# A depthwise 5x5 convolution as 24 tiles of 126 pixels, turned around the middle pixel, instead of 25 squares of 11x11

## What is computed

```python
k = jnp.transpose(kernel, (1, 2, 0))[:, :, None, :]
y = lax.conv_general_dilated(x, k, window_strides=(1, 1), padding='SAME',
                             dimension_numbers=('NHWC', 'HWIO', 'NHWC'), feature_group_count=ch)
return x + y
```

## Time and profile before

| | us |
|---|---|
| median of 3 runs | 827.06 |
| lowest, highest | 826.73, 827.2 |
| the profiled execution | 826.83 |
| its span | 825.0 |
| TensorE busy | 814.7 |
| VectorE busy | 670.8 |
| ScalarE busy | 619.6 |
| GpSimd busy | 591.9 |

### The profile page before, as it was taken

One profiled execution on the slowest core, in us unless ns is written; L12 is line 12 of the kernel. 1 busy time (PEld: TensorE's weight loads), 2 busy tenths in 40 slices (PEclk: granted clock), 3 DMA queues, 4 the chain that ended last, 5 costly groups with the idle time before them and its releaser, 6 DMA issues.

```text
span 825.0 us, 20812 instructions
## 1 busy us (share of the span) xinstructions
PE 814.7 (99%) x7200; PEld 814.5 (99%) x7200; DVE 670.8 (81%) x2118; ACT 619.6 (75%) x1538; POOL 591.9 (72%) x389
## 2 busy tenths in 40 slices
PE   6999999999999999999999999999999999999998
PEld 6999999999999999999999999999999999999998
DVE  6888888878788887878888888878888887888886
ACT  5777777777777777777777777777777777777775
POOL 6768577696775867858668677685775867758662
PEclk9999999999999999999999999999999999999999
DMA  9999999999999999999999999999999999999975
GB/s 364 414 388 402 354 395 375 376 381 367 402 371 376 384 371 395 376 368 400 355 382 398 368 400 363 373 397 356 401 372 378 353 404 384 377 365 405 363 317 227
DMA packets 28759, 309.29 MB, mean 375 GB/s; under 512 B 3184, under 2 KB 3312, under 8 KB 4208
## 3 DMA queue, kind: packets, MB, share of 16 engines
q1 hardware_dynamic: 28656, 307.98, 97.1%
HBM read 158.55 MB, written 149.42 MB: 373 GB/s over the span
## 4 chain that ended last, share of the span: by engine, by line
PE 99%; POOL 0%; DMA 0%; issue 0%; ACT 0%; DVE 0%; DVEq 0%
PE sums L419 66%; PE sums L415 33%; POOL matrix L237 0%; DMA first<-consts 0%; POOL expanded L228 0%; POOL taps L219 0%; POOL spare L216 0%; POOL taps L214 0%; ACT y_out L307 0%; DVE y_out L357 0%; DVEq L95 0%
## 5 line engine op out<-in xcount | busy, mean ns | idle before, releaser
L419 PE MATMUL sums<-matrix,x_high 121*128 121x240 f32 (+3 forms) x4800 | 814.2, 278 | 0.0
L419 PEld LDWEIGHTS sums<-matrix,x_high 121*128 121x128 f32 x4800 | 730.7, 192 | 0.0
L415 PE MATMUL sums<-matrix,x_low 121*128 121x240 f32 (+3 forms) x2400 | 665.8, 277 | 6.8 <-POOL matrix L237 6.8
L307 ACT ACTIVATE y_out<-sums 128x220 f32<-128x220 f32 (+6 forms) x1248 | 420.5, 376 | 194.3 <-PE sums L419 175.8
L357 DVE TENSOR_TENSOR y_out<-sums,y_out 128x60 f32<-128x60 f32 (+5 forms) x1824 | 358.8, 227 | 144.6 <-ACT y_out L307 62.6
L415 PEld LDWEIGHTS sums<-matrix,x_low 121*128 121x128 f32 x2400 | 460.4, 192 | 6.9 <-POOL matrix L237 6.8
L265 POOL TENSOR_TENSOR x_low<-x_in,x_high 121x640 fp32r<-121x640 f32 x190 | 320.7, 1710 | 119.0 <-DVE x_high L331 119.0
L340 DVE TENSOR_TENSOR x_low<-x_in,x_high 121x1280 fp32r<-121x1280 f32 (+1 forms) x194 | 290.2, 1497 | 2.2 <-ACT x_high L297 2.1
L297 ACT ACTIVATE x_high<-x_in 121x640 fp32r<-121x640 f32 (+1 forms) x288 | 263.6, 916 | 7.3 <-DMA x_in<-x 7.3
L253 POOL TENSOR_TENSOR matrix<-expanded,mask 121x600 fp32r<-121x600 f32 x95 | 157.9, 1662 | 92.4 <-PE sums L419 90.5
L331 DVE CAST x_high<-x_in 121x640 fp32r<-121x640 f32 x96 | 68.1, 710 | 3.8 <-DMA x_in<-x 3.3
(11 more groups left out here) (5 smaller groups left out, 0.6 us busy)
## 6 DMA issues: line engine op xcount, KB each, us to landing
x_in<-x SPq DMA_DIRECT2D x95, 1600.0 KB, 10.2
y<-y_out SPq DMA_DIRECT2D x95, 1520.0 KB, 13.2
rest<-later SPq DMA_DIRECT2D x1, 1150.0 KB, 12.1
x_in<-x SPq DMA_DIRECT2D x3, 320.0 KB, 3.6
y<-y_out SPq DMA_DIRECT2D x1, 852.5 KB, 3.6
x_in<-x SPq DMA_DIRECT2D x1, 640.0 KB, 6.1
y<-y_out SPq DMA_DIRECT2D x1, 365.0 KB, 2.3
y<-y_out SPq DMA_DIRECT2D x1, 302.5 KB, 2.7
```

The costliest lines, as they stand in the source:

```text
L307: act.activation(outputs(c, rows, cols), sums(c, t, rows, cols), ACT.Copy).then_inc(copied, 1)
L415: pe.matmul(target, x_low[c % SLOTS][0:PIXELS, at:at + IMAGES], window(c, strip, k, slice(HIGH, HIGH + 1)).squeeze(1), start=k == tile["sq ...
L419: product = pe.matmul(target, x_high[c % SLOTS][0:PIXELS, at:at + IMAGES], window(c, strip, k, slice(part, part + 1)).squeeze(1), start=Fa ...
```

## The change

The plane is cut into 24 tiles of 14x9 = 126 pixels instead of 25 squares of 121. Four quarters, each 28 x 27, turn around the middle pixel like the blades of a wheel; two hold lying tiles (FLAT, 9 rows by 14 columns), two standing ones (TALL, 14 by 9). The middle pixel itself, which no quarter covers, is a 127th pixel of one tile. So there are 72 matmuls a channel, 6912 in all, and two matrices a channel, one for each kind of tile. The columns of the moving operands sum up to 5270 a channel per matmul of the three, against 5396 before.

- Two tiles share a bank: 12 banks a channel, 12 copies, 14 seams of 1445 elements. wait_bank is as before, with 12 in place of 13.
- The input is 3072 columns a channel (in memory 3104 a row), in four pieces of 768. VectorE casts the first, ScalarE the three others; VectorE makes all four low parts. GpSimd makes none.
- GpSimd spreads the taps channel by channel, by two copies (200 and 150 elements), and multiplies four times 300 elements: high and low part for each of the two kinds. The mask is no longer computed but loaded (128 x 600 numbers, 300 KB, behind the first input piece). The tap splits have 200 elements instead of 100.
- The last channel's output is stored in two parts, 687.5 and 832.5 KB, instead of three.

The core of the diff; the lists of each engine:

```diff
-SQUARE = 11
-ACROSS = SIDE // SQUARE
-PIXELS = SQUARE * SQUARE
+LONG, SHORT = 14, 9
+PIXELS = LONG * SHORT
+QUARTERS = (
+    (FLAT, (0, 14), (0, 9, 18)),
+    (TALL, (0, 14), (28, 37, 46)),
+    (FLAT, (27, 41), (28, 37, 46)),
+    (TALL, (27, 41), (0, 9, 18)),
+)
+SHAPES = ((15, 20), (20, 15))
+ROWS, COLS = zip(*SHAPES)
+STORED = (20, 16)
+HIGH_AFTER = (2, 5, 7)
+CAST_AFTER = 2
+LOW_AFTER = (4, 5, 7, 9)
...
 # GpSimd
-            def make_matrix(c):
-                if c >= SLOTS:
-                    pool.wait_ge(sums_done, TILE_COUNT * (c - SLOTS + 1))
-                shape = [PIXELS, 2, REACH // TAPS, EXPANDED]
-                pool.tensor_tensor(
...
-            for c in range(1, CHANNELS):
-                if c % GROUP == 0:
-                    split_taps(c // GROUP)
-                    pool.wait_ge(matrix_step, c + 1)
-                    spread_taps((0, GROUP))
-                    pool.wait_ge(spread, c // GROUP + 2)
-                make_matrix(c)
-                for piece in range(HEADS):
-                    split_low(c, piece)
+            def make_matrix(c):
+                pool.wait_ge(spread_step, KINDS * (c + 1))
+                if c == 0:
+                    pool.wait_ge(masks_loaded, 16)
+                if c >= SLOTS:
+                    pool.wait_ge(sums_done, BANK_COUNT * (c - SLOTS + 1))
+                for kind in range(KINDS):
+                    shape = [whole, ROWS[kind] // TAPS, TAPS, COLS[kind]]
+                    for part in (HIGH, LOW):
+                        pool.tensor_tensor(
...
+            for c in range(CHANNELS):
+                if c % GROUP == 0:
+                    split_taps(c // GROUP)
+                spread_taps(c)
+                make_matrix(c)
...
 # VectorE
             for c in range(CHANNELS):
-                following = c + 1 < CHANNELS
-                add_seams(c, 0)
-                if following:
-                    cast_high(c + 1)
-                add_seams(c, 1)
-                add_seams(c, 2)
-                if following:
-                    split_low(c + 1, 2)
-                add_seams(c, 3)
-                if following:
-                    split_low(c + 1, 3)
-                add_seams(c, 4)
+                for t in range(BANK_COUNT):
+                    add_seams(c, t)
+                    if c + 1 < CHANNELS:
+                        if t == CAST_AFTER:
+                            cast_high(c + 1)
+                        if t in LOW_AFTER:
+                            split_low(c + 1, LOW_AFTER.index(t))
...
 # TensorE
-                pe.wait_ge(matrix_step, c + 2)
-                for t, tile in enumerate(TILES):
+                for t, bank in enumerate(PLAN):
+                    kind, quarter = bank["kind"], bank["quarter"]
+                    if t % (BANK_COUNT // PIECES) == 0:
+                        if quarter < KINDS:
+                            pe.wait_ge(matrix_step, 2 * KINDS * c + 2 * (kind + 1))
+                        pe.wait_ge(low_ready, PIECES * c + quarter + 1)
+                    wait_bank(c, t)
```

More of the change, by code:

```diff
@@ L81 @@
[L81 to L94, removed]
+TURNED = KINDS * FILTER
+HIGH_AFTER = (2, 5, 7)
+CAST_AFTER = 2
+LOW_AFTER = (4, 5, 7, 9)
+CONSTS = GROUP * TURNED + TURNED
+LATER = (GROUPS - 1) * GROUP * TURNED
@@ new lines, in rectangles, with plan_of_sums @@
+def rectangles(cells):
+    found, left = [], cells.copy()
+    while left.any():
+        y, x = np.argwhere(left)[0]
+        right = x
+        while right < SIDE and left[y, right]:
+            right += 1
+        bottom = y
+        while bottom < SIDE and left[bottom, x:right].all():
+            bottom += 1
+        left[y:bottom, x:right] = False
+        found.append(((int(y), int(bottom)), (int(x), int(right))))
+    return found
+def plan_of_sums(banks):
+    covered = np.zeros((SIDE, SIDE), bool)
+    earlier = []
+    for bank in banks:
+        cells = np.zeros((SIDE, SIDE), bool)
+        cells[slice(*bank["rows"]), slice(*bank["cols"])] = True
+        (bank["copy"],) = rectangles(cells & ~covered)
+        seams = sorted(rectangles(cells & covered), key=lambda r: (r[0][0] < r[0][1] and (
+            [n for n, e in enumerate(earlier) if meet(e, r)] or [-1])[-1]))
+        bank["adds"] = []
+        for seam in seams:
+            after = [n + 1 for n, e in enumerate(earlier) if meet(e, seam)]
+            bank["adds"].append((seam, after[-1] if after else 0))
+            earlier.append(seam)
+        covered |= cells
+    return len(earlier)
@@ L95, in build, with meet @@
+def meet(a, b):
+    return all(p[0] < q[1] and q[0] < p[1] for p, q in zip(a, b))
+PLAN = banks_of_plane()
+ADDS = plan_of_sums(PLAN)
+BANK_COUNT = len(PLAN)
+ADDS_BEFORE = [sum(len(b["adds"]) for b in PLAN[:n]) for n in range(BANK_COUNT + 1)]
+TOP_BANKS, TOP_ROWS = 6, min(b["rows"][0] for b in PLAN[6:])
+def build(nc, consts, masks, later, x, out):
     with ExitStack() as ctx:
@@ L105, in build @@
         y_out = [sbuf(f"y_out{i}", [P, OUT_COLS], F32) for i in range(Y_SLOTS)]
[L106 removed]
+        matrix = [[sbuf(f"matrix{i}_{k}", [P, 2, ROWS[k], STORED[k]], F32R) for k in range(KINDS)] for i in range(SLOTS)]
+        mask = sbuf("mask", [P, KINDS, CELLS], F32)
         first = sbuf("first", [P, CONSTS], F32)
         rest = sbuf("rest", [P, LATER], F32)
[L109 to L110 removed]
@@ L111, in build @@
-        expanded = sbuf("expanded", [P, GROUP, 2, EXPANDED], F32)
-        mask = sbuf("mask", [P, MATRIX], F32)
+        taps = sbuf("taps", [P, GROUP, KINDS, 2, FILTER], F32R)
+        spare = sbuf("spare", [P, GROUP, KINDS, FILTER], F32)
+        spread = [sbuf(f"spread{k}", [P, 2, TAPS * COLS[k]], F32) for k in range(KINDS)]
         warm = sbuf("warm", [P, 1], F32)
         psum = ctx.enter_context(nc.psum_tensor("sums", [P, BANKS, BANK], F32))
-        at = GROUP * FILTER
-        centre = first[0:PIXELS, at:at + FILTER]
@@ L118, in build @@
[L118 to L123, removed]
+        whole = PIXELS + 1
+        centre = first[0:whole, GROUP * TURNED:CONSTS].rearrange("p (k f) -> p k f", f=FILTER)
@@ new lines, in corners_of_tiles @@
+def corners_of_tiles():
+    for kind, along, across in QUARTERS:
+        for v in across:
+            for u in along:
+                yield (kind, v, u) if kind == FLAT else (kind, u, v)
+def lay_out_input(x):
+    plane = x.transpose(3, 1, 2, 0)
+    rows = np.zeros((CHANNELS, P, IN_PITCH), x.dtype)
+    for n, (kind, top, left) in enumerate(corners_of_tiles()):
+        high, wide = (SHORT, LONG) if kind == FLAT else (LONG, SHORT)
+        rows[:, :PIXELS, n * IMAGES:(n + 1) * IMAGES] = plane[:, top:top + high, left:left + wide].reshape(
+            CHANNELS, PIXELS, IMAGES)
+        if n == CENTRE_TILE:
+            rows[:, PIXELS, n * IMAGES:(n + 1) * IMAGES] = plane[:, CENTRE, CENTRE]
```

347 lines of the change are left out of this document (147 added, 200 removed).

## The result

The changed kernel took **842.16 us** (median of 4 runs, 841.52 to 843.0) against 827.13 of the kernel before: a ratio of 1.0183, 95% interval 1.0165 to 1.02. The forecast was 797 us, the range 786 to 822. The profiled execution took 843.0 us, its span is 841.2.

What follows compares the result with a forecast made beforehand. TensorE was taken as the bound, at a price per matmul: 826.83 us - 32.6 (matmuls) + 1.0 (start) + 1.5 (end) = 796.7, forecast as 797 us since the median lay 0.23 higher; range 786 to 822.

Steps and rivals of the forecast that it cites:

- Matmuls: TensorE: 7200 matmuls become 6912 at an unchanged 113.15 ns each, 782.1 us against 814.7, so 32.6 us less.
- Start: Chain to the first matmul: longer tap steps and two copies instead of one spread, +1.0 us, between +0.5 and +2.
- End: After the last matmul: a last store of 832.5 KB takes 3.6 us instead of 2.3, plus one add; +1.5 us.
- VectorE, ScalarE, GpSimd: Work beside TensorE: VectorE 6.7, ScalarE under 6.45, GpSimd 4.8 of 8.15 us a channel; hidden, cost nothing.
- what they share: VectorE and GpSimd take turns: 9.2 us a channel, 7.9 with hand-overs saving 0.13 each, against 8.15; cost nothing.
- transfers: DMA: input falls from 1600 to 1536 KB a channel; 384 GB/s asked for, hidden, cost nothing.
- Rival 1: VectorE and GpSimd hold each other up, TensorE waits for "added"; 836 us if half the hand-overs save; chance 0.11.
- form without any saved hand-over: VectorE and GpSimd taking turns with no 0.13 us saved: 9.2 us a channel, 898 us; chance 0.01.
- Rival 2: TensorE: time follows the columns, 5270 against 5396 a plane, 8.29 us a channel, 811 us; chance 0.06.
- Rival 3: DMA: transfers are the bound, 303.2 MB at the earlier mean rate of 375 GB/s, 810 us; chance 0.05.
- Rival 4: TensorE: new windows step otherwise; half the tiles at 120 ns give 821 us, at 110 give 786; slow side's chance 0.06.
- the prediction's saving: VectorE and GpSimd: each hand-over between them saves 0.13 us, up to ten a channel, 9.2 us becoming 7.9.

## Why the prediction was wrong, point by point

- *Matmuls.* This is the step that failed: "the width hardly matters ... I take the step as a price per matmul", with bounds of 110 and 120 ns "since most of the new windows lie among the old widths". The premise was true of the rows read and no more. Of the old windows of 16 columns 13 in 15 begin at column 0 of rows 20 apart: 60 groups for 15 rows, and by the fit 60 groups stream in 110 ns, just under the load that each matmul brings anyway. Of the 24 new windows 16 touch 64 to 72. The right quantity was neither the width nor the number of matmuls, but the groups of 16 bytes that a window touches, and the diff shows them: rows of 14 numbers stored 16 apart, rows of 18 stored 20 apart and windows from column 2. The term measured +12.7 us instead of -32.6, a miss of 45.3: 6912 x (119.70 - 113.15). With start and end (+1.2, -0.2 against the forecast) that is the whole difference of 46.3 between 843.0, the profiled execution, and 796.7.
- A sign of it stood in the trace of the kernel before, outside the rows read. Three windows of 13 x 16 follow each other; the middle one begins at column 1 and touches 65 groups instead of 52. Its three matmuls take 0.35 us, its neighbours' 0.34 and 0.33; over the channels its steps are 118 to 119 ns, those of the neighbours' last two 109 to 113:

```profile
405.65 0.28 PE L415 MATMUL sums<-matrix,x_low 121*128 121x208 f32 x1
...
405.99 0.29 PE L415 MATMUL sums<-matrix,x_low 121*128 121x208 f32 x1
...
406.34 0.27 PE L415 MATMUL sums<-matrix,x_low 121*128 121x208 f32 x1
...
406.67 0.27 PE L415 MATMUL sums<-matrix,x_low 121*128 121x182 f32 x1
```

- The expected gain was there to be had: with the rows stored without gaps, the mean is 113.50 ns and the time 799.38, 2.4 us above the forecast. That the old mean fits so well is partly luck: it comes from other windows, and most windows step at the load's 110 to 114 ns in both kernels.
- *Start.* Mis-sized: +2.2 us in the profiled execution, +1.0 forecast, because the constants landed 0.28 later and three of GpSimd's steps beside VectorE's took longer than alone. The other runs with the same start had +1.3 to +1.6.
- *End.* From the last matmul's start to the end of the span 5.1 us, 1.3 more than before (3.8); +1.5 was forecast. The last store of 832.5 KB landed in 3.4 us, 3.6 were assumed.
- *VectorE, ScalarE, GpSimd, what they share, transfers.* Right in that all of it stayed hidden. The version at 799.38 us is the harder proof, since its channel is as short as the forecast's; TensorE waits for nothing there but the start, with VectorE at 85% (81% in the changed kernel, where over 85 was a sign of being right).
- Rival 1 (VectorE becomes the bound) did not occur: no wait for "added" or "matrix_step" after the start, in the changed kernel or in the version at 799.38. Its form without any saved hand-over gave 898 us, from 9.2 us a channel, and that sum was too high: with the least durations in the version at 799.38 (a cast of 0.55, four low parts of 0.94, four products of 0.73, two copies of 0.31, and 0.45 for the tap steps) it is 8.3 us, against 8.17 that a channel took there. That form was also the rule of the Trainium skill, page "SBUF — State Buffer", section "SBUF: two separate sides"; 8.3 against 8.17 is too close for these runs to tell its full lock from the prediction's saving.
- Rival 2 (columns) fell with rows 18 and 14 apart: same columns, 43 us less. Rival 3 (transfers): the mean rate was 362 GB/s in the changed kernel and 382 in the faster version at a share of 97 and 98%, so the share is no ceiling.
- Rival 4 was what happened, "by no rule of columns", and its sign, steps that differ by tile, is what the timeline shows. It had no mechanism, a chance of 0.06 and a price of 116.6 ns; the mean of 119.70 lies above that, and windows at 130 lie above the bound of 120.
- The formula that the prediction set against the row, N/2.4 + 2.5 ns (the Trainium skill, "TensorE: Matmul & The Clock Gate", section "Back-to-back issue gap"), gives 107.5 for 252 columns; the timelines show 130 with gaps (400.84 to 401.23, three matmuls) and 115 without (400.20 to 400.43, two). That section calls the formula the isolated gap and says that in a stream of loads and matmuls both set the spacing, so it was no rule for this kernel. The trace agrees with neither the formula nor a price per matmul, but with the larger of load and groups.

## What to carry to other kernels

A price per instruction read from a trace holds for the layouts in that trace: ask what it hides under, and how far the new shapes are from that cover. For float32r matmuls like these count the groups of 16 bytes that the moving operand's window touches, row by row with its start column; store rows without gaps where windows span the full width, and start the others at a multiple of four. Then see if the stream fits under the load of the stationary operand.

## What the runs showed of the hardware

- At the full clock a matmul's step was the larger of about 112 ns (put down to its load) and about 10 + 1.67 ns for each group of 16 bytes of the moving operand. The same 18 x 12 window took 110 ns from column 0 and 130 from column 2; 15 x 16 took 113 from column 0 and 135 from column 1. The Trainium skill speaks of 16-byte cachelines on "Advanced Engine Details and Errata", section "SBUF Cachelines", with a penalty where accesses do not share one; it gives no price, and none for TensorE.
- One kind of window does not follow: in the kernel before, 15 rows of 14 numbers from column 3 touch 75 groups, and a matmul of theirs took 111 to 119 ns and not 135: one such tile took 0.36 us (400.24 to 400.60), the two others in a channel 0.33 to 0.34. Why was not tried.
- The further apart the rows, the slower the slow windows: some 3 ns a matmul from 16 to 20 (18 x 14) and from 20 to 24 (14 x 18).
- A short matmul gives nothing back while each one brings a load: 96 columns stepped in 0.05 us and the next matmul paid 0.17.
- With half of the columns gone from two matmuls in three, TensorE has no stretch of full clock on record and stayed at 213 ns a step for the whole run, though busy for 99% of it; in the eleven other kernels the full clock was granted, at the latest 6.5 us after the first matmul. What made the difference is open.
